# A four-layer graph network on one core: in the third edge stage VectorE finishes messages ahead of its additions, and loads one-hots that the second edge stage stored in DRAM

## What is computed

```python
# second layer (second edge stage)
msg = relu(h[src] + edge_attr_32 @ We + be)
aggr = segment_sum(msg, dst, N)
# third layer (third edge stage)
hn = mlp(h, node_ln, node_W)                    # layernorm, matmul, leaky relu (0.01)
he = mlp(edge_attr_64, edge_ln, edge_W)
emb_edge = mlp(concatenate([hn[src], he]), red_ln, red_W)
z = (segment_sum(emb_edge, dst, N) + emb_local) / (deg + 1)
```

## Time and profile before

| | |
|---|---|
| median of 3 runs (lowest, highest) | 6001.68 us (5985.96, 6005.3) |
| the profiled execution | 5993.58 us, span 5991.8 us |
| busy over the span | TensorE 4384.6, VectorE 4119.1, GpSimd 3245.5, ScalarE 2010.8 us |
| second edge stage | about 1477 to 2533 us of the span |
| third edge stage | about 2640 to 3915 us |
| granted TensorE clock, mean | 0.866 |

### The profile page before, as it was taken

How to read it: one execution, slowest core, us unless ns; L and a number is a source line. 1 busy time by engine, 2 the same in 40 slices (tenths; PEclk the granted TensorE clock), 3 DMA queues, 4 the chain that set the end, 5 groups by cost and what they waited for, 6 DMA issues and landing times. The chain is left out here.

```text
span 5991.8 us, 104214 instructions
## 1 busy us (share of the span) xinstructions
PE 4384.6 (73%) x29528; PEld 2839.4 (47%) x29528; DVE 4119.1 (69%) x7954; ACT 2010.8 (34%) x6556; POOL 3245.5 (54%) x2950
## 2 busy tenths in 40 slices
PE   3999999997666767656666666637777777639999
PEld 2444444443333333435444445524444444439998
DVE  5776777667565666556666666646666666789998
ACT  2566666664000000023333333300000000047775
POOL 4666666662555555434444444345666656425554
PEclk6999999998788888758788888868999989869998
DMA  4333333331111111111111111123333344311111
GB/s 112 95 89 89 94 94 91 90 92 38 40 37 39 40 36 41 25 33 42 38 39 39 40 40 40 31 66 107 109 109 108 109 116 110 100 36 48 50 48 34
DMA packets 493104, 393.99 MB, mean 66 GB/s; under 512 B 346007, under 2 KB 379168, under 8 KB 492904
## 3 DMA queue, kind: packets, MB, share of 16 engines
q1 hardware_dynamic: 395496, 303.53, 17.8%
q0 software_dynamic: 90560, 83.37, 7.7%
q10 hardware_dynamic: 6976, 6.23, 0.3%
HBM read 355.34 MB, written 37.42 MB: 66 GB/s over the span
## 5 line engine op out<-in xcount | busy, mean ns | idle before, releaser
L1090 POOL DMA_INDIRECT edge_src_rows<-table_wh,edge_gather_idx x806 | 871.5, 1081 | 487.0 <-issue 230.5
L947 POOL DMA_INDIRECT edge3a_src_rows<-table_h,edge3a_gather_idx x808 | 762.2, 943 | 561.8 <-issue 315.1
L2138 PE MATMUL edge3a_z_ps<-Wz,edge3a_both_ends_t 128*128 128x396 f32 x1616 | 700.8, 582 | 354.8 <-DVE edge3a_terms L2231 310.5
L947 POOL DMA_INDIRECT table_cat<-table_hn,table_gather_idx x592 | 597.2, 1009 | 644.6 <-PE edge_cat_t_ps L1816 347.7
L1120 PE MATMUL edge_sums_ps<-edge_onehot_src,edge_halves 128*128 128x512 bf16 x4840 | 888.4, 330 | 46.6 <-issue 36.6
L1496 POOL DMA_INDIRECT edge_src_rows<-table_h,edge_gather_idx x608 | 609.5, 1002 | 533.8 <-PE edge_msg_ps L1528 186.7
L2231 DVE SCALAR_TENSOR_TENSOR edge3a_terms<-edge3a_z_ps,att_z 128x792 f32<-128x792 f32 x404 | 386.0, 977 | 406.5 <-DMA edge_edge_attr<-in_ea 222.1
L2138 PEld LDWEIGHTS edge3a_z_ps<-Wz,edge3a_both_ends_t 128*128 128x128 f32 x1616 | 335.3, 218 | 665.0 <-DVE edge3a_terms L2231 356.8
L1120 PEld LDWEIGHTS edge_sums_ps<-edge_onehot_src,edge_halves 128*128 128x128 f16 x4840 | 385.1, 97 | 474.1 <-issue 65.7
L2550 PE MATMUL edge3b_sums_ps<-edge3b_onehot,edge3b_weighted 128*128 128x128 f32 x4848 | 572.2, 278 | 6.3 <-DVE layers_accT L2588 4.0
L2550 PEld LDWEIGHTS edge3b_sums_ps<-edge3b_onehot,edge3b_weighted 128*128 128x128 f32 x4848 | 552.9, 193 | 12.1 <-DVE layers_accT L2588 4.3
(11 more groups left out here) (370 smaller groups left out, 8464.2 us busy)
## 6 DMA issues: line engine op xcount, KB each, us to landing
edge_dst_row<-in_dst_row SPq DMA_DIRECT2D x102, 512.0 KB
edge3a_dst_row<-in_dst_row SPq DMA_DIRECT2D x102, 512.0 KB
edge_window<-table_wh_parts SPq DMA_DIRECT2D x816, 48.8 KB
edge3a_window<-table_h SPq DMA_DIRECT2D x816, 32.0 KB
edge_edge_attr<-in_ea SPq DMA_DIRECT2D x101, 256.0 KB
kept_rows<-edge3a_src_rows SPq DMA_DIRECT2D x101, 256.0 KB
edge3b_src_rows<-kept_rows SPq DMA_DIRECT2D x101, 256.0 KB
edge_edge_attr<-in_ea SPq DMA_DIRECT2D x101, 128.0 KB
```

The source lines that it names most:

```text
L947: nc.gpsimd.indirect_dma_start(self.slot(b, j), None, self.table[:, :], bass.IndirectOffsetOnAxis(ap=self.idx[b][:, j:j + 1], axis=0)).the ...
L1090: nc.gpsimd.indirect_dma_start(g[q][:, j, :], None, k.t_wh[:, :], bass.IndirectOffsetOnAxis(ap=idx[q][:, j:j + 1], axis=0)).then_inc(gathe ...
L2138: mm = pe.matmul(zp[q % 2][:, i, 0:H * ZH], hcT[h][:, j * P:(j + 1) * P], k.Wz[:, :], start=True, stop=True)
```

## The change

The second edge stage stores each batch's one-hot to a new DRAM tensor of [102, 128, 1024] floats, from ScalarE's queue, behind the relu of the batch; VectorE's next one-hot in the same buffer waits for the store. In the third edge stage VectorE makes no one-hots: SyncE loads them, each behind the sums that used the buffer before, and TensorE waits for the load. VectorE's order becomes (take 0), edge_row(n), message(n - 1), (take 1), add(n - 2). TensorE's `sum_up` now waits inside: before its first matmul for the first four additions of the batch before, before its fifth for the last.

```diff
@@ edge1, ScalarE @@
+                def keep(n, h):
+                    act.wait_ge(oh_ready, n + 1)
+                    act.dma_start(k.onehots[bass.ds(n, 1)].rearrange("a p e -> (a p) e"),
+                                  oh[h][:, :, :].rearrange("p b w -> p (b w)")).then_inc(oh_kept[h], 16)
...
+                keep(0, 0)
+                keep(1, 1)
...
                             if live(GROUP * gi + p + 2):
                                 relu(*two)
+                                keep(GROUP * gi + p + 2, p % 2)
...
+                act.wait_ge(oh_kept[0], 16 * (USED - USED // 2))
+                act.wait_ge(oh_kept[1], 16 * (USED // 2))
@@ edge1, VectorE @@
-                def onehot_of(n, h):
+                def onehot_of(n, h, kept=None):
+                    if kept is not None:
+                        dve.wait_ge(oh_kept[h], 16 * kept)
...
-                                onehot_of(n + 2, h)
+                                onehot_of(n + 2, h, 2 * gi + p // 2 + 1)
@@ edge2, SyncE @@
+                def hots(n, h):
+                    wait_past(sp, sums_ready, 2 * n - 2)
+                    sp.dma_start(oh[h][:, :, :].rearrange("p b w -> p (b w)"),
+                                 k.onehots[bass.ds(n, 1)].rearrange("a p e -> (a p) e")).then_inc(oh_loaded[h], 16)
+
+                hots(0, 0)
+                hots(1, 1)
...
+                        if not isinstance(t, int) or t > 2:
+                            hots(2 * t + h - 4, h)
                         if used_batch(t, h + 1) and not (isinstance(t, int) and 2 * t + h + 1 < 4):
...
+                for n in range(USED - 4, USED):
+                    hots(n, n % 2)
@@ edge2, TensorE @@
-                def sum_up(n, h):
+                def sum_up(n, h, tt):
                     pe.wait_ge(msg_ready, n)
-                    pe.wait_ge(oh_ready, n)
+                    pe.wait_ge(oh_loaded[h], 16 * (tt + 1))
                     for j in range(B):
+                        if j == 0:
+                            wait_past(pe, added[B // 2 - 1], n - 1)
+                        if j == B // 2:
+                            pe.wait_ge(added[B - 1], n + 1)
...
-                            if not (first and h == 1):
-                                pe.wait_ge(added[B - 1], n)
-                            sum_up(n - 1, 1 - h)
+                            sum_up(n - 1, 1 - h, t - 1 + h)
@@ edge2, VectorE @@
-                dve.tensor_copy(fixed[:, 0:P], k.row0[:, :]).then_inc(row_ready, 1)
...
+                        if b == TAKEN:
+                            take(m, 0)
                         edge_row(n, b)
                         if not (first and h == 0):
-
-                            onehot(dve, k, oh[1 - h][:, :, :], t - 1 + h, 1 - h, row).then_inc(oh_ready, 1)
+                            message(n - 1, 1 - h)
                         if b == TAKEN:
-                            take(m, 0)
+                            take(m, 1)
                         if not first:
                             add(n - 2, h, t - 1, m + (b == TAKEN), due(t, m, b))
...
-                        if b == TAKEN:
-                            take(m, 1)
-                        if not (first and h == 0):
-                            message(n - 1, 1 - h)
@@ build @@
+    k.onehots = dram("dst_onehots", (BATCHES, P, ROWS))
```

More of the change, by code:

```diff
@@ L1450, in edge1 @@
         added = [c.sem(f"added{j}") for j in range(B)]
+        oh_kept = [c.sem(f"onehot_kept{h}") for h in (0, 1)]
         (oh_ready, m_ready, msg_ready, sums_ready, hot_ready, hot_used, rowsT_ready, prepared,
@@ L1684, in edge2 @@
         (hep_ready, sq1, std1_ready, inv1, he_sc, he_b, cat_ready, catT_ready, rp_ready,
-         sq2, std2_ready, inv2, u_sc, u_b, oh_ready, msg_ready, sums_ready, ones_ready) = c.sems(
+         sq2, std2_ready, inv2, u_sc, u_b, msg_ready, sums_ready, ones_ready) = c.sems(
             "he_in_psum", "squares1_done", "std1_ready", "inverse1_done", "he_scaled", "he_shifted",
             "cat_ready", "cat_t_ready", "msg_in_psum", "squares2_done", "std2_ready",
-            "inverse2_done", "msg_scaled", "msg_shifted", "onehot_ready", "msg_ready", "sums_in_psum",
+            "inverse2_done", "msg_scaled", "msg_shifted", "msg_ready", "sums_in_psum",
             "ones_ready")
+        oh_loaded = [c.sem(f"onehot_loaded{h}") for h in (0, 1)]
         added = [c.sem(f"added{j}") for j in range(B)]
@@ L1710, in edge2 @@
         by_bank = catTp[:, :, :].rearrange("p i e -> p (i e)")
-        row, ec, rc = fixed[:, 0:P].unsqueeze(1), fixed[:, P:P + HALF], fixed[:, 2 * P:2 * P + D]
+        ec, rc = fixed[:, P:P + HALF], fixed[:, 2 * P:2 * P + D]
         with nc.Block() as block:
@@ L1839, in body @@
                         if not (first and h == 0):
-                            if not (first and h == 1):
-                                pe.wait_ge(added[B - 1], n)
-                            sum_up(n - 1, 1 - h)
+                            sum_up(n - 1, 1 - h, t - 1 + h)
                 by_parity(pe, body)
-                pe.wait_ge(added[B - 1], USED + 1)
-                sum_up(USED, 0)
+                sum_up(USED, 0, PAIRS - 1)
             @block.scalar
@@ L1891, in _ @@
                 dve.memset(msg[1][:, :, D], 1.0).then_inc(ones_ready, 1)
-                dve.wait_ge(row_ready, 3)
+                dve.wait_ge(row_ready, 2)
                 step = Chain(dve, prep)
@@ L2006, in body @@
                                 hot(0, i)
-                        if b == TAKEN:
-                            take(m, 1)
-                        if not (first and h == 0):
-                            message(n - 1, 1 - h)
                 by_parity(dve, body)
-                onehot(dve, k, oh[0][:, :, :], PAIRS - 1, 0, row).then_inc(oh_ready, 1)
+                message(USED, 0)
                 add(USED - 1, 1, PAIRS - 2)
-                message(USED, 0)
                 add(USED, 0, PAIRS - 1)
```

## The result

The changed kernel takes 6017.19 us (median of 20 runs, 6002.83 to 6043.28), the kernel before, measured beside it, 5998.70 (20 runs, 5975.29 to 6018.05): a ratio of 1.0032, 95% interval 1.0019 to 1.0045. It is slower by 18 us. The forecast said slower and 6040, which is 38 to 40 us more than before, so the measured change is less than half of it. By the prediction's own limit (5984 to 6020 is the same) 6017 still counts as no change; only the interval of the 20 runs lies clear of 1.

What follows compares the result with a forecast made beforehand. It took TensorE reports held until a gather's end to bound the kernel. Terms -6 -5 +7 +29 +15 = +40 on 5993.58 gave 6034, adjusted to the median 6042, stated as 6040; own range 6005 to 6080, overall 5850 to 6095.

Steps and rivals of the forecast that it cites:

- (e): Third stage: SyncE's one-hot loads lengthen the gather issues they fall beside, 0.4 us in each of 72 windows, +29 us.
- (b): Third stage, message ahead of additions: TensorE's earlier work stays held in gather windows, 0; in the gather-free end, -5 us.
- (g): Second stage: VectorE's one-hot waits for the store of two batches before, some 20 us earlier, so 0.
- The hold: Third stage: TensorE results finished late in a GpSimd gather are reported only at its end, in nearly every round.
- rival B: Third stage: TensorE issues early enough to escape late reports, second gather window 10.7 us; -194, total 5848; chance 0.32.
- (a): Third stage: the one-hot's 1.21 us a batch leaves VectorE, worth 0 under gathers, -6 us after the last gather.
- (c): Third stage, third window: message and edge_row precede the second take, and more rounds may run TensorE at 1.2 GHz; +7 us.
- C: Third stage: window 2 shrinks by 1.9 us, but the third gather's choose is seen 0.9 later; -24, 6018; chance 0.20.
- (f): Second stage: ScalarE's stores each wait at most 1.3 us for a one-hot, and ScalarE is little busy; 0.
- (h): Second stage: ScalarE's stores beside gather issues lengthen the windows, 0.2 us in each of 75, +15 us.
- A: The forecast itself, both stages: reports stay held to the gather's end; 6040 us, range 6005 to 6080, chance 0.42.

Runs made afterwards that it cites:

- reorder_only: Against the kernel before: only the third stage's new VectorE order and split wait, one-hots still made by VectorE, no stores or loads; 5969.64 us, ratio 0.9950.

## Why the prediction was right and wrong

That most windows end with a late report of TensorE was read rightly. The sum was not right: 18.5 us were measured where it had +40, and its terms were off in both directions. Three steps failed: (e), +29 in the third stage by longer gather issues, which did not get longer; (b), 0 in the windows, where the new order gave some 10 us; and (g), the wait on the store put at 0, which cost some 21 us.

- **The hold** ("what TensorE finishes late in a gather is reported only at the gather's end"): a wait in the row of gathers brings the reports forward, and with plain DMAs they aren't late; so far it is shown. As a rule it is too wide, since in the kernel before the msg_ps reports come at once 6.1 us into a gather. The round kept its shape, and rival B (5848) did not come.
- **(a), the one-hot is worth 0 under the gathers, 6 us in the end**: right, 1285.0 against 1286.2 us without and with it, and 4 to 5 us in the end.
- **(b), 0 in windows 1 and 2, -5 in the end**: the end is right. In the windows it is a miss by 0.35 and 0.4 us in the medians. The order moved the transposes up, from 9.9 to 5.1 us into the gather, and by my reading they come out among the first of the held reports instead of behind those of the sums. Added up, from the second round on, the first windows gave 11.5 us and the second ones 4.7. The order alone (reorder_only) was 28 us faster in the medians, where (b) and (c) together had +2; its profile has 12 us of that in the rounds (1230.2 to 1217.8) and 7 in the end. With VectorE's own one-hots it is C that happens in window 2 (11.09 us).
- **(c), +7**: the third windows cost 4.8 us more, 0.2 x 24 (and the first three windows of the loop 3.5). The second half of choose took over 4 us in 18 of 25 rounds, before in 13 (mean 4.35 against 3.88 us), the way of running at 1.2 GHz that (c) had named.
- **(e), +29 for loads beside gather issues**: this is the step that failed in the third stage. The mean issue fell from 1011 to 998 ns, and from the first gather issue to the last the stage took 7.9 us less, where (c) and (e) had 36 more. It was read from two long issues of the earlier trace rows that stood beside SyncE's; in the changed kernel an issue as long stands beside none, and the loads' own neighbours are short. By the medians of two kernels the loads do cost 21.6 us, but not by that mechanism, and I can't say by which.
- **(f), 0**: right as a wait of ScalarE, but the store stands behind the relu, and that is what (g) missed.
- **(g), 0 for the wait on the store**: this is the step that failed in the second stage. "Some 20 us earlier" was counted from when VectorE had made the one-hot. The store is issued behind a relu that waits for a held report, 11.2 us later in the median, which leaves 5.8 us of which the store needs 3.7; the wait was 71.5 us in 25 places. Storing ahead of the relu gave back some 21 us. The prediction had named the price ("a late store would count in full"), had VectorE waiting for onehot_kept among its signs of being wrong, and had not looked at what ScalarE's queue is waiting for.
- **(h), +15 by longer issues**: the size lies within the 0 to 20 us that stores without a waiter may cost, the mechanism is not shown: issues over 1.1 us in the second stage became fewer (97 before, 73 after).
- **The sum**: forecast +15 and +25, measured +27 and -18 in the profile, +18.5 in the medians. That 6017 lies in A's own range of 6005 to 6080 is luck in part, errors of opposite sign. It is also rival C's number (6018, no change that can be told), and that is luck too: C had window 2 shrink by 1.9 us, and in the changed kernel it shrank by 0.4.

## What to carry to other kernels

Where GpSimd gathers with indirect DMAs beside TensorE, look at when TensorE's results are seen, not at when they end: here, moving work earlier under a gather bought next to nothing while the report stayed in, and a short gap in the gathers was worth more than the work removed. A store that frees a buffer must be placed by what stands ahead of it on its queue, not by when its data are ready. A part of a change can be better than the whole: try the parts singly.

## What the chip showed that I had not expected

- TensorE's reports are late by up to 6 us and more under GpSimd's indirect DMAs (1.25 us apart, eight in a row) and by 0.1 us under plain DMAs of the same queue. ScalarE's report was not held where TensorE's was (3210.04 to 3210.13). A wait of some 2 us in the row lets them out: 5998.75 to 5711.28 us with such a wait in two stages and the new order.
- The hold isn't there in every part of a row of gathers: behind a pause it stayed away for about 4 us, and msg_ps was reported at once 6.1 us into a gather of the kernel before. What starts it is open.
- A 512 KB store from ScalarE's queue frees its buffer 3.7 us after issue. Stores and loads of 101 one-hots that nobody waits for cost some 22 to 42 us together.
